# A chunked linear-attention layer on one core: the running state as 128x128 blocks of eight heads in place of 32-row strips

## What is computed

```python
xn = layernorm(x)
q, k, v = silu(xn @ Wq), silu(xn @ Wk), silu(xn @ Wv)      # 16 heads of 16 channels
# linear attention with a decay per head, in chunks of the sequence; per head:
scores  = (q_chunk @ k_chunk.T) * D                        # D: decays, lower triangle
o       = scores @ v_chunk + (q_chunk @ S) * q_decay
S       = chunk_decay * S + (k_chunk * k_decay).T @ v_chunk # the running state, 16x16 per head
o = rmsnorm_per_head(o * sigmoid(gate)) * norm_w           # gate = xn @ Wg1 @ Wg2
s = o @ Wo
g = silu(fp8_round(xn * scale) @ fp8_round(W2 * scale1) / (scale * scale1))
out = x + s * g
```

## Time and profile before

| | |
|---|---|
| median of 3 runs | 150.11 us (150.04 to 150.51) |
| the profiled execution | 149.64 us, its span 147.9 us |
| TensorE busy | 125.7 us, 85% of the span |
| TensorE weight loads | 105.7 us, 71% |
| VectorE busy | 104.2 us, 70% |
| ScalarE busy | 74.1 us, 50% |
| GpSimd busy | 73.9 us, 50% |

### The profile page before, as it was taken

How to read it: one execution, slowest core, us unless ns; L and a number is a source line. 1 busy time by engine, 2 the same in 40 slices (tenths; PEclk the granted TensorE clock), 3 DMA queues, 4 the chain that set the end, 5 groups by cost and what they waited for, 6 DMA issues and landing times.

```text
span 147.9 us, 7195 instructions
## 1 busy us (share of the span) xinstructions
PE 125.7 (85%) x3126; PEld 105.7 (71%) x3126; DVE 104.2 (70%) x276; ACT 74.1 (50%) x140; POOL 73.9 (50%) x115
## 2 busy tenths in 40 slices
PE   4977889454899899999999998799999999849771
PEld 4876687332798689778967896679878976638650
DVE  0949999865669588947993799188937961954663
ACT  4497668556466547554655465547552753001000
POOL 6955875992633566536652665256516630130030
PEclk9999999995599999999999999999999999995999
DMA  2869100000000000200020002000200020020004
GB/s 85 276 187 358 46 0 4 4 4 0 7 0 4 4 4 0 75 4 4 2 75 4 4 0 75 4 4 4 78 0 4 7 75 4 0 75 4 4 0 142
DMA packets 6847, 6.06 MB, mean 41 GB/s; under 512 B 1376, under 2 KB 6816, under 8 KB 6816
## 3 DMA queue, kind: packets, MB, share of 16 engines
q1 hardware_dynamic: 6816, 5.60, 11.7%
HBM read 3.50 MB, written 2.10 MB: 38 GB/s over the span
## 4 chain that ended last, share of the span: by engine, by line
PE 66%; DVE 18%; issue 6%; ACT 4%; POOL 4%; DVEq 0%; POOLq 0%; ACTq 0%
PE b_o L1073 8%; PE b_q L1117 7%; PE b_o L1057 5%; PE b_q L923 5%; PE b_s L1018 4%; PE b_s L989 3%; DVE probs L653 3%; PE b_k L999 3%; PE b_x L909 2%; PE b_v L936 2%; PE b_v L1123 2%; PE b_v L939 2%; PE b_v L937 2%; PE b_k L937 2%; PE b_k L936 2%
## 5 line engine op out<-in xcount | busy, mean ns | idle before, releaser
L337 POOL TENSOR_TENSOR e_sum<-e_y,e_magic 128x512 f32<-128x512 f32 x8 | 10.2, 1275 | 20.5 <-DVE e_magic L638 20.5
L686 DVE SCALAR_TENSOR_TENSOR og<-gate_tanh,b_o 128x512 f32<-128x512 f32 x8 | 5.5, 688 | 18.3 <-PE b_o L1073 18.3
L1073 PE MATMUL b_o<-probs,v_par 64*32 64x64 f32 x1024 | 15.8, 228 | 2.2 <-issue 2.0
L1073 PEld LDWEIGHTS b_o<-probs,v_par 64*32 64x32 f32 x1024 | 10.3, 108 | 7.2 <-issue 5.9
L345 POOL TENSOR_TENSOR qd<-q_silu,q_decay 128x512 f32<-128x512 f32 x8 | 10.4, 1299 | 9.5 <-ACT q_silu L473 9.5
L1117 PE MATMUL b_q<-wo_scaled,on 128*128 128x256 f32 x56 | 14.2, 394 | 0.8 <-DVE on L738 0.8
L373 POOL TENSOR_TENSOR y<-sg,x_sb 128x512 f32<-128x512 f32 x7 | 9.0, 1290 | 11.4 <-DVE sg L759 11.4
L529 ACT ACTIVATE b_x<-b_x,minus 128x64 f32<-128x64 f32 x8 | 2.3, 288 | 23.4 <-DVE b_x L711 23.4
L355 POOL TENSOR_TENSOR own_mid<-state_mid,head_parity 128x128 f32<-128x128 f32 x8 | 3.2, 399 | 18.9 <-DVE state_mid L666 16.1
L1117 PEld LDWEIGHTS b_q<-wo_scaled,on 128*128 128x128 f32 x56 | 10.0, 189 | 2.7 <-DVE on L738 1.0
L653 DVE TENSOR_TENSOR probs<-b_o,decay_mask 128x512 f32<-128x512 f32 x16 | 10.3, 685 | 1.7 <-PE b_o L1018 1.5
(11 more groups left out here) (166 smaller groups left out, 385.3 us busy)
## 6 DMA issues: line engine op xcount, KB each, us to landing
out_dram<-y SPq DMA_DIRECT2D x7, 256.0 KB, 2.2
x_sb<-in_L_attn_x_dram SPq DMA_DIRECT2D x4, 384.0 KB, 5.6
x_sb<-in_L_attn_x_dram SPq DMA_DIRECT2D x2, 256.0 KB, 3.6
w_f<-in_L_attn_Wq_dram SPq DMA_DIRECT2D x1, 256.0 KB, 3.3
w_f<-in_L_attn_Wk_dram SPq DMA_DIRECT2D x1, 256.0 KB, 3.6
w_f<-in_L_attn_Wv_dram SPq DMA_DIRECT2D x1, 256.0 KB, 4.2
w_f<-in_L_ffn_input_dram SPq DMA_DIRECT2D x1, 256.0 KB, 3.6
wo_f<-in_L_attn_Wo_dram SPq DMA_DIRECT2D x1, 256.0 KB, 6.0
```

Source lines behind the costliest of these rows:

```text
L337: g.tensor_tensor(e4_sum[:], e4_y[:, n % 2], e4_magic[:, n % 2], ALU.add).then_inc(s_e4sum, 1)
L1073: mm = t.matmul(ps_o[32 * r:32 * r + 32, c, z:z + C], v_par[rows, u, blk:blk + 2 * E], probs[rows, r, s, i:i + C], start=(half == 0 and s ...
```

## The change

The state is kept as full blocks of 128 x 128: all eight heads of a half against all eight, for each half and batch, where before each group of 32 partitions had 32 columns. `state_steps` gives 128 key columns and 8 x 16 value columns to one matmul, so r falls away: 8 matmuls (4 in steps 6 and 7) of 64 rows, 128 output rows and 128 columns. `from_state` does a half and batch in one matmul of 128 rows, 128 output rows and 64 columns: 4 per share in place of 16. The tiles `state_mid`, `state_end`, `own_mid`, `own_end` and the part of PSUM behind `ps_u` have four times the columns, and so do the operations on them on VectorE and GpSimd; their number is the same. The mask is now `own_head`, eight columns that leave a partition its own head of eight. `ps_u` fills banks `b_q` and `b_k` whole, so the head sums of the last step move to free columns of `b_s`, and they wait for the masks that read the scores there (`s_probs`) and no longer for `s_mid`.

```diff
-        state_mid = sb("state_mid", [P, PAIRS, KH, S, 2 * E])
-        state_end = sb("state_end", [P, PAIRS, KH, S, 2 * E])
-        own_mid = sb("own_mid", [P, 2, KH, S, 2 * E])
-        own_end = sb("own_end", [P, 2, PAIRS, KH, S, 2 * E])
+        state_mid = sb("state_mid", [P, PAIRS, KH, S, P])
+        state_end = sb("state_end", [P, PAIRS, KH, S, P])
+        own_mid = sb("own_mid", [P, 2, KH, S, P])
+        own_end = sb("own_end", [P, 2, PAIRS, KH, S, P])
...
-        ps_u = [b[:, 0:W // 4].rearrange("p (k s e) -> p k s e", k=KH, s=S) for b in (b_q, b_k)]
+        ps_u = [b[:].rearrange("p (k s e) -> p k s e", k=KH, s=S) for b in (b_q, b_k)]
...
-        ps_sum_last = b_k[:, W // 2:W // 2 + C]
+        ps_sum_last = b_s[:, D:D + C]
...
-                return g.tensor_tensor(dst.rearrange("p k s (b e) -> p (k s) b e", b=2), src.rearrange("p k s (b e) -> p (k s) b e", b=2),
-                                       head_parity[:].unsqueeze(1).unsqueeze(3).broadcast_to([P, KH * S, 2, E]), ALU.mult)
+                return g.tensor_tensor(dst.rearrange("p k s (h e) -> p (k s) h e", h=HH), src.rearrange("p k s (h e) -> p (k s) h e", h=HH),
+                                       own_head[:].unsqueeze(1).unsqueeze(3).broadcast_to([P, KH * S, HH, E]), ALU.mult)
...
-                        for r in range(4):
-                            for c in range(2 if pos(n) < NB - 1 else 1):
-                                rows = slice(c * C, c * C + C)
-                                heads = v_par[rows, u].rearrange("p (q z) -> p q z", q=2)[:, :, 0:W].rearrange("p q (a z) -> p a q z", a=H)
-                                mm = t.matmul(u_ps[c][32 * r:32 * r + 32, half, s], kd[rows, u, s, half * P + 32 * r:half * P + 32 * r + 32],
-                                              heads[:, s * HH + half * 4 + r, :, 0:E], start=True, stop=True, skip_group_check=True)
+                        for c in range(2 if pos(n) < NB - 1 else 1):
+                            rows = slice(c * C, c * C + C)
+                            heads = v_par[rows, u].rearrange("p (q z) -> p q z", q=2)[:, :, 0:W].rearrange("p q (a z) -> p a q z", a=H)
+                            first = s * HH + half * 4
+                            mm = t.matmul(u_ps[c][:, half, s], kd[rows, u, s, half * P:half * P + P],
+                                          heads[:, first:first + 4, :, 0:E], start=(half == 0 and s == 0), stop=True, skip_group_check=True)
...
-                        for r in range(4):
-                            rows = slice(32 * r, 32 * r + 32)
-                            st = own_end[rows, (pos(n) - 1) % 2, pair(n), half, s] if c == 0 else own_mid[rows, u, half, s]
-                            z = (half * S + s) * C
-                            t.matmul(ps_o[rows, c, z:z + C], st, qd[rows, u, half, s * P + c * C:s * P + c * C + C],
-                                     start=False, stop=False, skip_group_check=True)
+                        st = own_end[:, (pos(n) - 1) % 2, pair(n), half, s] if c == 0 else own_mid[:, u, half, s]
+                        z = (half * S + s) * C
+                        t.matmul(ps_o[:, c, z:z + C], st, qd[:, u, half, s * P + c * C:s * P + c * C + C],
+                                 start=False, stop=False, skip_group_check=True)
...
-                    pe.wait_ge(s_mid, STEPS)
+                    pe.wait_ge(s_probs, 4 * STEPS)
```

## The result

The changed kernel took 152.33 us (median of 18 runs, 151.46 to 153.95), the kernel before 150.52 in its 18 runs (148.05 to 152.54). The ratio is 1.0203, with a 95% interval from 1.0159 to 1.0247: slower, and whether by more or by less than 2% the interval leaves open. The kernel before spreads over 4.5 us from run to run, and the ratio rests on its quicker runs, so it is larger than the ratio of the two medians, 1.012. The profiled execution took 153.95 us, its span 152.2; it was the longest of the 18.

The account below looks back on a forecast made before the run. TensorE's own stream was taken as the bound in steps 1 to 6. Terms of +7.7 and -5.2 us gave +2.5: 149.64 to 152.1 profiled, 152.6 as median; forecast 150.6 to 154.5 (chance 0.46), range 147.8 to 157.5.

Parts of the forecast that it names:

- the last step: Step 7: shares and from_chunk -1.5 us without the stall, keep-warm matmuls -1.0 from a higher clock; -2.5 us in all.
- State steps: state_steps on TensorE: halves side by side, 55 ns a record, 1.0 us for 0.69, +0.3 a step; +0.6 in step 6.
- rival 1: The two chunks of state_steps do not run side by side: 1.76 us a group, 157.0 us in all; chance 0.17.
- Shares: from_state on TensorE: 110 ns a record, set by weight load; +0.8 us a step with both shares, +0.4 in step 1.
- The wait before transpose_k: TensorE waits for VectorE's wider state sums (state_end) about 0.1 us in each of steps 2 to 5.
- Step 0: VectorE is the chain in the first step; its wider copy and pair of sums add 0.8 us.
- GpSimd: Wider mask operations, 1.06 to 1.27 us each, hidden by idle time; cost nothing, except 0.1 us in step 7.
- Stalls: Unexplained TensorE stalls, paced by blocks of some 256 instructions per 3.9 us, go with fewer records; steps 1 to 6 save 2.7 us.
- rival 2: The stalls stay, as instruction count does not pace them: 2.7 us back, 3.2 in step 7; 158.5 us; chance 0.09.
- the 1.0 us that I took for the clock: Ten keep-warm records in step 7 run without the clock drop once the stall goes; 1.0 us saved of at most 1.15.
- rival 3: Moving columns set the shares' pace: 55 ns a record, 5.2 us less; 147.4 us, faster than before; chance 0.15.
- rival 4: Half the stalls stay or later sums hold up transpose_k by 0.3 us: 154 to 156; or step-0 slack: 151.5; chance 0.13.

Follow-up runs that it names:

- the probe: Changed kernel with a tail of unread identity matmuls of several forms, then 384 of 32x32; full-weight records 112 ns apart, the burst in pieces of 128 every 3.45 to 4.00 us.
- the kernel with narrow sums: Changed kernel's large matmuls, but VectorE and GpSimd work on 64 state columns as before, part of the arithmetic left out; 151.12 us, ratio 1.019 to the kernel before.
- the kernel with blocks of 64x64: Kernel before with the state in 64x64 blocks of four heads, 16 matmuls per state step and 8 per share; 144.53 us, ratio 0.9745.
- the kernel with both small: Changed kernel with state steps and shares as small 32x32 matmuls again, only sums and masks wide; 150.73 us, ratio 1.0035 to the kernel before.
- the small state steps: Changed kernel with state_steps as 32 matmuls of 32x32 again, on the diagonal blocks; 151.03 us, ratio 1.0181 to the kernel before.
- the two with matmuls in the gap: Six keep-warm matmuls added before the last step's first from_chunk: in the changed kernel 153.73 us, ratio 1.0391; in the kernel before 147.78 us, ratio 0.9993.

## Why the prediction was right, point by point

**Direction and size.** 152.6 us was forecast and 152.33 measured, +2.5 forecast and +1.8 between the medians of 18 runs each, +3.1 by the ratio. In steps 0 to 6 the sum came out near (+5.0 forecast, +4.4 between the two profiled executions), but there two terms were too small and offset one another; for the last step it was wrong. The two profiled executions differ by 4.3 us, not by 2.5. That the medians differ by less goes with how often the clock was low in either kernel, as told below, which the forecast did not foresee. So the closeness of the final number is in good part luck.

**State steps: right in kind, 0.1 us too low.** The halves run side by side at 55 ns, so rival 1 falls, and with it the doubt whether half-array tiles do what the scores' tiles do; the Trainium skill ("TensorEngine Tiling (Array Packing)", Available Configurations) lists the form with two tiles, and this trace agrees that they work side by side. The group takes 1.10 us from 76.34 to 77.44, not 1.0. The first record starts 0.21 us ahead of the second and the gate starts 0.21 behind the last: the change of tiles costs some 0.1 us at each end where I allowed 0.12 in all. Step 6, 8 records with nothing beside them:

```profile
122.52 1.09 PE b_q L1039 x8
```

against 1.0 forecast and 0.39 before. (Before, a pause of 0.15 us stands behind the 0.39, so that from start to start it is 0.60 there and the growth 0.5 us.)

**Shares: right.** 1.84 us against 1.81, both from start to start: records 112 ns apart, and 0.05 us for the change of tiles, as allowed. The 110 ns came from 128 moving columns, and the probe gives them and 64 the same pace. The growth is 0.8 us a step, as forecast.

**VectorE: the wait was twice what I took.** The wait before transpose_k is 0.7 us in four steps, 0.18 each, where I had 0.1; the kernel with narrow sums prices it at 0.23 a step. A pair of sums is 0.87 us behind one another, as forecast; what I gave too little was the way from TensorE's last record to VectorE's first sum and from the last sum back. Step 0 grew by 0.65 us, not 0.8. The chain there:

```profile
26.15 0.70 DVE state_mid L663
...
26.88 0.87 DVE state_end L678 x2
```

The two are 0.40 us each longer than in the earlier trace rows, as forecast, and 0.15 of it is taken up further on.

**GpSimd: nothing, as forecast.** own_mid takes 1058 ns, at the lower of my bounds, and nobody waits for it.

**Stalls: gone in steps 1 to 6, as forecast, but worth more than their rows say.** The rows "issue" give 2.7 us in steps 1 to 6, of which 2.1 lie in steps 2 to 5. Such a row begins only where the last record is modelled to end, some 0.3 us after it started. From start to start, the part of from_chunk in step 3 that holds the stall of 0.65 us took 1.33 us and the same part without one takes 0.38, so that the stall cost 0.95. Without it step 3 would be 13.92 us long (14.87 - 0.95; the kernel with blocks of 64x64 has 13.93 there), and by that length steps 2 to 5 lost 59.09 - 4 x 13.92 = 3.4 us to the supply. The account then closes: 4 x (0.40 for the state steps + 0.80 for the shares + 0.23 for the wait) = +5.7, less 3.4 is +2.3, and +2.4 was measured. I had +4.8 less 2.1 there. Both terms were too small, by 0.9 and by 1.3 us, and the errors took each other back.

The trace of before has one more stall, of 0.4 us, in front of the state steps of the last step (line 1038; it ends at 128.10, where the second interval of the earlier trace rows begins). The prediction's 4.6 us leave it out, and it was wrong to say for rival 2 that the stalls sit only in lines 1057 and 1073.

The two halves of the change are not worth the same in this. Starting from the kernel with both small, the small shares go first to large ones: 61.36 - 59.40 = +2.0 us in steps 2 to 5. The state steps go first: 58.89 - 59.40 = -0.5, since their 0.4 us a step buys off the stalls. Once either is done, the other finds few stalls left to save.

**The last step: -2.5 forecast, -0.45 found.** This is the step that failed. Its chain in the changed kernel, against the earlier trace rows, and the clock at its end:

```profile
133.32 1.17 PE b_o L1072 x72
134.50 0.84 issue
135.34 1.89 PE b_o L1056 x16
...
137.61 2.29 PE b_v L1122 x10
```

```profile
137.60:139.90 2.30, 2.30 (x16) 2.08 (x18) 1.53 (x4) 0.63 (x1) 0.00 (x0) 0.53 0.28 94
```

Two terms were off. First, the stall shrank from 1.94 to 0.84 us and did not go. It now stands before the shares and not between them: from the start of the scores at 129.54 to the stall at 134.50 TensorE goes through 188 records (64 of the scores, 4, 16 and 8 of the next three groups, 96 of from_chunk) in 4.96 us, and the 128 records that one block holds came no faster than every 3.45 us in the probe. That the shares are smaller in number comes too late for it. The stretch from scores to keep-warm is 8.07 us for 8.72, -0.65 where I had -1.5. Second, the clock fell in the same place as before, to 0.53, and the ten keep-warm records took 2.29 us, so the 1.0 us that I took for the clock did not come at all. I had read the fall of before as a result of the long stall. That reading falls, as the stall alone does not bring it about: the kernel with both matmuls small stalls for 1.67 us at 132.54 and its clock stays up. The size of the term was about right, had the clock stayed up: the keep-warm records, head sums and keep-warm records behind take 3.46 us before, 3.68 in the changed kernel and 2.43 in the kernel with narrow sums. What decides whether the clock falls there stays open.

**The granted clock differs from run to run, and times go with it.** Each run has a mean granted clock, and the runs group by it. Mean times in us, with the number of runs (of before the 40 that stood beside the experiments, not beside the 18 of the changed kernel):

| mean granted clock | before | after |
|---|---|---|
| 0.973 to 0.977 | 147.6 (10) | 152.0 (9) |
| 0.963 to 0.966 | 150.0 (11) | 153.1 (6) |
| 0.940 to 0.955 | 151.1 (19) | 152.2 (3) |

Where the clock is high in both, the change costs 4.4 us, well over the forecast. The lengths give as much for steps 0 to 6: +0.65, +0.49, +2.40 and +0.86 are +4.4. The end takes 20.7 to 21.6 us in the experiments whose clock stays up there or nearly so, whatever the form of the matmuls, and 22.04 and 22.07 in the two with matmuls in the gap. In the middle group, from which the two profiled executions come, the means differ by 3.1 only, so that this agreement is not tight. The kernel before had half of its runs in the lowest group, the changed one a sixth, and that gives back part of the 4.4 in the medians. Which part of a run is slow in that group is not shown: no profile of one was taken of either kernel. The one profiled execution of the group, that of the small state steps (mean 0.952), has its lower clock in the first steps and none at the end:

```profile
29.20:42.80 13.60, 11.09 (x176) 8.65 (x176) 8.41 (x25) 7.18 (x14) 8.98 (x10) 0.50 0.01 4
128.00:140.00 12.00, 10.28 (x297) 8.35 (x297) 8.76 (x23) 1.75 (x4) 2.28 (x2) 1.00 0.08 26
```

So the rarer low clock can't be credited to the last step. Of the 12 runs of the kernel before with matmuls in the gap none is in the lowest group, against 7 of the 17 beside them, which chance alone would give about once in 80 times. That hints that what TensorE does there matters to the clock; it does not show how.

**Range and rivals.** The median of 152.33 us lies in the forecast's 150.6 to 154.5. Rivals 1, 2 and 3 are refuted by rows: 55 ns for the halves, no stalls in steps 1 to 6 and pauses that end behind the packets of instructions, and the same pace at 64 and 128 moving columns. Of rival 4, the mixtures, a part came true: a stall stayed in the last step, and the later sums hold up transpose_k in each of steps 2 to 5.

## What to carry to other kernels

Small matmuls on a tiled array met two limits here beside the array: instructions came in blocks of 256 every 3.5 to 4 us, and a record with 128 weight columns cost 112 ns however few columns moved. Make blocks larger until the stalls end, and no further: here 64x64 ended them in all steps but the last at no cost in array time, while 128x128 bought the same relief with seven eighths of its products thrown away and 1.2 us more of TensorE's time a step (0.8 in the shares, 0.4 in the state steps). Price a stall from start to start, not by its idle row, which misses 0.2 to 0.3 us of each. Try the middle size before the extreme one, and count how many instructions lie in the densest 4 us before pricing either.

## What the runs showed of the hardware that was not expected

- Small matmuls back to back come in pieces of 128 records every 3.45 to 4.00 us, with TensorE's granted clock at 1.00 or 0.50 alike. That is 27 to 31 ns on average for a record, weight load counted in, where within a piece a 32x32 record takes 10 ns at clock 1.00 (1.27 us for 128) and 15 at 0.50.
- A pause of this kind ends 1.2 to 1.6 us after a packet of the instruction queue is complete, in all 34 cases of the ten traces.
- Records with 128x128 float32 weights start 112 ns apart, with 32 or 64 moving columns as with 128. With 64 weight columns it is 58 ns and with 32 weight columns 56, at 64 moving columns.
- Going from full to half-array tiles and back costs some 0.2 us in all, measured in the middle of a step.
- The same kernel has runs whose mean granted clock is 0.94 and others with 0.977, and 3.5 us lie between their mean times (151.1 and 147.6).
